# A gated cross-attention block with an fp8 feed-forward on one core: attention stage rebuilt, mean shift added at the output, w_linear's waits moved

## What is computed

```
query  = ctx @ Wq.T + bq                      # ctx: (4, 256, 128)
key    = ctx @ Wk.T + bk
attn   = softmax(query @ key.T)               # (4, 256, 256)
x = x + tanh(g_xattn) * (layernorm(x) @ attn.T)          # x: (4, 256 tokens, 256)
h = layernorm(x)
act = gelu(fp8(h) @ fp8(w_gating[0])) * (fp8(h) @ fp8(w_gating[1]))
x = x + tanh(g_ffn) * (fp8(act) @ fp8(w_linear))         # hidden size 1024
```

## Time and profile before

| what | us |
|---|---|
| median of 3 timed runs (56.16 to 57.09) | 56.71 |
| span of the profiled execution | 54.7 |
| PE busy | 43.6 (80%) |
| DVE busy | 39.6 (72%) |
| POOL busy | 30.7 (56%) |
| ACT busy | 29.6 (54%) |

### The profile page before, as it was taken

One profiled execution on the slowest core, in us unless ns is written; L12 is line 12 of the kernel. 1 busy time (PEld: TensorE's weight loads), 2 busy tenths in 40 slices (PEclk: granted clock), 3 DMA queues, 4 the chain that ended last, 5 costly groups with the idle time before them and its releaser, 6 DMA issues.

```text
span 54.7 us, 874 instructions
## 1 busy us (share of the span) xinstructions
PE 43.6 (80%) x245; PEld 28.7 (53%) x245; DVE 39.6 (72%) x113; ACT 29.6 (54%) x67; POOL 30.7 (56%) x57
## 2 busy tenths in 40 slices
PE   1999999919999401998289999999999999998200
PEld 0338888707888101983234364664564668884000
DVE  1110099999960059998999999949998599889930
ACT  4413636597897930633148966697444693555000
POOL 4109700079992009889898889888884079302200
PEclk9999999999999999999999999999999999999997
DMA  0597999999999700000000000000000003520063
GB/s 0 142 296 175 361 337 263 192 201 204 196 200 279 310 9 0 0 0 0 6 0 0 0 12 0 6 0 0 0 6 0 0 0 113 181 102 0 0 252 131
DMA packets 3461, 5.43 MB, mean 99 GB/s; under 512 B 384, under 2 KB 1792, under 8 KB 3456
## 3 DMA queue, kind: packets, MB, share of 16 engines
q1 hardware_dynamic: 2880, 4.85, 27.0%
q0 software_dynamic: 576, 0.52, 10.3%
HBM read 5.90 MB, written 1.05 MB: 127 GB/s over the span
## 4 chain that ended last, share of the span: by engine, by line
PE 36%; DMA 23%; DVE 13%; SPq 11%; issue 5%; ACT 5%; POOL 1%; DVEq 1%; ACTq 0%
DMA wl<-w_linear 23%; PE bank L686 12%; PE bank L711 11%; PE bank L692 11%; SPq L227 5%; SPq L219 3%; DVE x L483 3%; DVE aq L527 3%; DVE st L488 2%; SPq L217 2%; ACT gl L397 2%; DVE xh L502 2%; PE bank L668 2%; POOL r L274 1%; ACT ys L405 1%
## 5 line engine op out<-in xcount | busy, mean ns | idle before, releaser
L397 ACT ACTIVATE gl<-bank 128x512 bf16<-128x512 f32 (+1 forms) x20 | 10.0, 509 | 6.4 <-PE bank L686 6.4
L518 DVE SCALAR_TENSOR_TENSOR ap<-bank,gl 128x512 f16<-128x512 f32 (+1 forms) x20 | 11.5, 577 | 2.2 <-PE bank L692 1.5
L711 PE MATMUL bank<-wl_q,aq 128*128 128x256 bf16 x64 | 10.1, 273 | 0.8 <-DVE aq L527 0.6
L686 PE MATMUL bank<-xq,wg 128*128 128x512 fp8e4 (+1 forms) x40 | 10.2, 337 | 0.2 <-ACT xq L388 0.2
L692 PE MATMUL bank<-xq,wg 128*128 128x512 fp8e4 (+1 forms) x40 | 10.2, 337 | 0.0
L527 DVE TENSOR_SCALAR aq<-ap 128x512 uint16<-128x512 uint16 (+1 forms) x20 | 8.5, 430 | 0.0
L711 PEld LDWEIGHTS bank<-wl_q,aq 128*128 128x128 f16 x64 | 5.8, 97 | 4.7 <-DVE aq L527 2.3
L646 PE MATMUL bank<-attnT,xT_sb 128*128 128x256 f32 x32 | 8.1, 385 | 0.0
L302 POOL TENSOR_TENSOR wl_sum<-wl_big,wl 128x256 f32<-128x256 f32 x8 | 5.9, 734 | 0.5
L618 PE MATMUL bank<-ident,attn 128*128 128x128 f32 x16 | 2.5, 280 | 4.5 <-POOL attn L283 3.3
L307 POOL TENSOR_TENSOR wl_q<-wl_sum,wl_big 128x256 bf16<-128x256 f32 x8 | 5.8, 728 | 0.5
(11 more groups left out here) (54 smaller groups left out, 69.8 us busy)
## 6 DMA issues: line engine op xcount, KB each, us to landing
x_sb<-x SPq DMA_DIRECT2D x4, 256.0 KB, 5.0
wl<-w_linear SPq DMA_DIRECT2D x2, 512.0 KB, 10.0
xT_sb<-xT SPq DMA_DIRECT2D x4, 256.0 KB, 11.0
out<-yo SPq DMA_DIRECT2D x6, 128.0 KB, 1.9
wg<-w_gating POOLq DMA_DIRECT2D x4, 128.0 KB, 10.1
par<-params_ctxT SPq DMA_DIRECT2D x1, 258.0 KB, 2.7
par<-params_ctxT SPq DMA_DIRECT2D x1, 256.0 KB, 4.5
out<-yo SPq DMA_DIRECT2D x1, 256.0 KB, 2.0
```

Of the source, the lines that this page charges most:

```text
L397: nc.scalar.activation(gl[:, s % 2, toks], gate_b[s % 2][:, toks], ACT.Gelu_apprx_tanh).then_inc(gelu_ready, 1)
L518: nc.vector.scalar_tensor_tensor(ap[:, s % NAP, toks], up_b[s % 2][:, toks], ACT_SCALE, gl[:, s % 2, toks], ALU.mult, ALU.mult).then_inc(p ...
L686: mm = nc.tensor.matmul(gate_b[s % 2][:, toks], wg8[:, c, k, 0, o:o + P], xq[:, g, k, toks], start=(k == 0), stop=(k == KC - 1))
L711: mm = nc.tensor.matmul(halves(y_b[g][i])[:, t], aq[:, s % NAQ, m:m + P], wl_q[:, j], start=(j == 0 and t == 0), stop=(j == HT - 1), skip_ ...
```

## The change

- SyncE loads x and xT of batches 0 and 1, then of 2 and 3, then both halves of w_linear. GpSimd's w_gating loads wait for xT of batch 0.
- The projections of batches 2 and 3 are one product of 512 columns each. k of batches 0 and 1 leaves PSUM on VectorE, one `k_out` of 512 columns and all of q on ScalarE.
- `bn_stats` runs once per batch over the two halves interleaved (512 elements); its even and odd parts are the two tokens' statistics, so no `bn_aggr` follows. The variance is taken from the sum of squares by 1/D.
- `xs` is gone: x2 = s1 * product + x, without the shift. nms1 is added at the output: as the bias of `scale_out`, which now writes each half by itself, and for three halves by `shift_x2` on GpSimd.
- Normalisation of attn: batch 0 on VectorE, 1 to 3 on GpSimd. ve2 and nm2 of batches 2 and 3 are made on GpSimd.
- `wl_constant` runs on ScalarE, for two slices at a time, after the second `xq_out` and among the first gelus. `wl_exponents` stand behind `norm2(1)` and behind step 2 of the feed-forward.
- The orders on all engines are written anew; attend is no longer split around other work.

```diff
-            for b in range(B):
+            for b in (0, 1):
                 sp.dma_start(x_sb[:, b], x[b]).then_inc(s_x[b], 16)
-
-            def load_w_linear(h):
+            for b in (0, 1):
+                sp.dma_start(xT_sb[:, b], xT[b]).then_inc(s_xT[b], 16)
+            for b in (2, 3):
+                sp.dma_start(x_sb[:, b], x[b]).then_inc(s_x[b], 16)
+            for b in (2, 3):
+                sp.dma_start(xT_sb[:, b], xT[b]).then_inc(s_xT[b], 16)
+            for h in range(2):
                 half = slice(h * HT // 2, (h + 1) * HT // 2)
                 sp.dma_start(wl32[:, half], w_linear[:, half]).then_inc(s_wl[h], 16)
-
-            load_w_linear(0)
-            for b in range(B):
-                sp.dma_start(xT_sb[:, b], xT[b]).then_inc(s_xT[b], 16)
-            load_w_linear(1)
...
+            def scales1(h):
+
+                bs = slice(2 * h, 2 * h + 2)
+                pool.wait_ge(st1_ready, 2 * h + 2)
+                nc.gpsimd.tensor_scalar(ve1[:, bs], st1[:, bs, :, 2], 1.0 / D, EPS, ALU.mult,
+                                        ALU.add).then_inc(ve1_ready, 1)
+                pool.wait_ge(ve1_ready, h + 1)
+                nc.gpsimd.tensor_tensor(r1[:, bs], ve1[:, bs], neg_half[:, bs], ALU.pow).then_inc(r1_ready, 1)
+                pool.wait_ge(r1_ready, h + 1)
                 pool.wait_ge(ntg_ready, 1)
-                nc.gpsimd.tensor_scalar(nr1[:, :, :], r1[:, :, :], ntg[:, 0:1], None, ALU.mult).then_inc(nr1_ready, 1)
-                nc.gpsimd.tensor_scalar(s1[:, :, :], r1[:, :, :], tg[:, 0:1], None, ALU.mult).then_inc(s1_ready, 1)
+                nc.gpsimd.tensor_scalar(s1[:, bs], r1[:, bs], tg[:, 0:1], 1.0, ALU.mult,
+                                        ALU.mult).then_inc(s1_ready, 1)
...
+            def shifts1():
+                nc.gpsimd.tensor_scalar(nr1[:, :, :], r1[:, :, :], ntg[:, 0:1], 1.0, ALU.mult,
+                                        ALU.mult).then_inc(nr1_ready, 1)
                 pool.wait_ge(nr1_ready, 1)
-                nc.gpsimd.tensor_tensor(nms1[:, :, :], nr1[:, :, :], mv1[:, :, :, 0], ALU.mult).then_inc(nms1_ready, 1)
+                nc.gpsimd.tensor_tensor(nms1[:, :, :], nr1[:, :, :], st1[:, :, :, 1], ALU.mult).then_inc(nms1_ready, 1)
 
             def rstd2(b):
+                if b >= 2:
+                    pool.wait_ge(st2_ready, b + 1)
+                    nc.gpsimd.tensor_scalar(ve2[:, b], st2[:, b, :, 2], 1.0 / D, EPS, ALU.mult,
+                                            ALU.add).then_inc(ve2_ready, 1)
+                    nc.gpsimd.tensor_scalar(nm2[:, b], st2[:, b, :, 1], -1.0, 1.0, ALU.mult,
+                                            ALU.mult).then_inc(nm2_ready, 1)
                 pool.wait_ge(ve2_ready, b + 1)
...
+            def shift_x2(b, t):
+
+                pool.wait_ge(nms1_ready, 1)
+                pool.wait_ge(x2_ready, LT * b + t + 1)
+                nc.gpsimd.tensor_scalar(x2s[:, b, t], x2[:, b, t], 1.0, nms1[:, b, t:t + 1], ALU.mult,
+                                        ALU.add).then_inc(x2s_ready, 1)
+
...
-            def wl_constant(c):
-                pool.wait_ge(wl_exp_ready, 2 * c * WLC // HT + 1)
-                nc.gpsimd.tensor_scalar(wl_tile(wl_big, c), wl_tile(wl_exp, c), WL_SLOPE, WL_OFFSET, ALU.mult,
-                                        ALU.add).then_inc(wl_big_ready, 1)
-
             def wl_up(c):
-                pool.wait_ge(wl_big_ready, c + 1)
+                pool.wait_ge(wl_big_ready, c // WLB + 1)
...
             def round_wl(c):
-                wl_constant(c)
                 wl_up(c)
                 wl_down(c)
 
-
-            pool.wait_ge(s_ctx[1], 16)
+            nc.gpsimd.memset(wl_offset[:, :], WL_OFFSET).then_inc(offset_ready, 1)
+            pool.wait_ge(s_xT[0], 16)
             for c in range(NWG):
                 load_w_gating(c)
             pool.wait_ge(consts_ready, 1)
-            scales1()
-            shift_x(0)
-            shift_x(1)
-            wl_constant(0)
-            normalise(B - 1)
-            wl_up(0)
+            scales1(0)
+            normalise(1)
+            scales1(1)
+            normalise(2)
+            normalise(3)
             rstd2(0)
-            wl_down(0)
-            wl_constant(1)
             rstd2(1)
-            wl_up(1)
-            wl_down(1)
-            round_wl(2)
+            round_wl(0)
             rstd2(2)
-            round_wl(3)
-            wl_constant(4)
-            wl_up(4)
+            round_wl(1)
             rstd2(3)
-            wl_down(4)
-            for c in range(5, HT // WLC):
+            shifts1()
+            for c in range(2, HT):
                 round_wl(c)
+            for b, t in ((2, 0), (3, 0), (3, 1)):
+                shift_x2(b, t)
             for k in range(LT * GB):
                 add_residual(k)
-
-            pool.wait_ge(scaled_ready, GB + 1)
+            pool.wait_ge(scaled_ready, LT * GB + 1)
             nc.gpsimd.tensor_tensor(yo[:, 2, 1], ys[:, 2, 1], x2[:, 2, 1], ALU.add).then_inc(pool_y_ready, 1)
...
+            def wl_constant(h):
+
+                act.wait_ge(wl_exp_ready, h // 2 + 1)
+                rows = slice(WLB * h, WLB * (h + 1))
+                nc.scalar.activation(wl_big[:, rows].rearrange("p j d -> p (j d)"),
+                                     wl_exp[:, rows].rearrange("p j d -> p (j d)"), ACT.Identity,
+                                     bias=wl_offset[:, 0:1], scale=WL_SLOPE).then_inc(wl_big_ready, 1)
+
+            def scale_out(b, t):
                 g, i = divmod(b, GB)
                 act.wait_ge(ffn2_done, last_step(b) + 1)
-                if b == 0:
+                if b == 0 and t == 0:
                     act.wait_ge(yscale_ready, 1)
-                nc.scalar.activation(ys[:, b].rearrange("p t d -> p (t d)"), y_b[g][i][:, :], ACT.Copy,
+                    act.wait_ge(nms1_ready, 1)
+                nc.scalar.activation(ys[:, b, t], halves(y_b[g][i])[:, t], ACT.Identity, bias=nms1[:, b, t:t + 1],
                                      scale=yscale[:, 0:1]).then_inc(scaled_ready, 1)
...
             q_out(0)
-            k_out(0)
             q_out(1)
-            k_out(1)
+            exps(0)
             q_out(2)
             k_out(2)
-            exps(0)
-            q_out(3)
-            k_out(3)
             exps(1)
             attn_out(0)
             exps(2)
+            attn_out(1)
             exps(3)
-            attn_out(1)
+            nc.scalar.activation(table[:, :], tg[:, 0:1], ACT.Gelu_apprx_tanh)
             attn_out(2)
-
-            nc.scalar.activation(table[:, :], tg[:, 0:1], ACT.Gelu_apprx_tanh)
-            shift_x(2)
+            xq_out(0)
             attn_out(3)
-            shift_x(3)
-            xq_out(0)
             xq_out(1)
+            act.wait_ge(offset_ready, 1)
+            wl_constant(0)
             for s in range(S):
                 gelu(s)
+                if s == 0:
+                    wl_constant(1)
+                if s in (3, 4):
+                    wl_constant(s - 1)
                 if s == X_AFTER[0] - 2:
                     norm2(2)
...
+            def k_out(c):
+                b0, b1 = PROJ[c]
+                dve.wait_ge(k_done, c + 1)
+                nc.vector.tensor_scalar(kT[:, b0 * L:b1 * L], k_b[c][:, 0:(b1 - b0) * L], bk, None,
+                                        ALU.add).then_inc(k01_ready, 1)
...
             def stats1(b):
                 dve.wait_ge(s_x[b], 16)
-                for t in range(LT):
-                    nc.vector.bn_stats(st1[:, b, t], x_sb[:, b, t]).then_inc(st1_ready, 1)
-                for t in range(LT):
-                    dve.wait_ge(st1_ready, LT * b + t + 1)
-                    nc.vector.bn_aggr(mv1[:, b, t], st1[:, b, t]).then_inc(mv1_ready, 1)
+                nc.vector.bn_stats(st1[:, b].rearrange("p t s -> p (t s)"),
+                                   x_sb[:, b].rearrange("p t d -> p d t")).then_inc(st1_ready, 1)
...
+                dve.wait_ge(s1_ready, b // 2 + 1)
                 for t in range(LT):
-                    nc.vector.scalar_tensor_tensor(x2[:, b, t], halves(pv_b[b % 2])[:, t], s1[:, b, t:t + 1], xs[:, b, t],
-                                                   ALU.mult, ALU.add).then_inc(x2_ready, 1)
...
-            def stats2(b, t):
-                dve.wait_ge(x2_ready, LT * b + t + 1)
-                nc.vector.bn_stats(st2[:, b, t], x2[:, b, t]).then_inc(st2_ready, 1)
-
-            def moments2(b):
-                for t in range(LT):
-                    dve.wait_ge(st2_ready, LT * b + t + 1)
-                    nc.vector.bn_aggr(mv2[:, b, t], st2[:, b, t]).then_inc(mv2_ready, 1)
-                dve.wait_ge(mv2_ready, LT * (b + 1))
...
+                    nc.vector.scalar_tensor_tensor(x2[:, b, t], halves(pv_b[b % 2])[:, t], s1[:, b, t:t + 1],
+                                                   x_sb[:, b, t], ALU.mult, ALU.add).then_inc(x2_ready, 1)
+
+            def stats2(b):
```

(98 more changed lines are left out.)

107 lines of the change are left out of this document (45 added, 62 removed).

## The result

| | before | after |
|---|---|---|
| median, us | 56.64 (56.16 to 57.09, 4 runs) | 60.16 (59.52 to 60.38, 4 runs) |
| ratio after / before | 1 | 1.062, 95% interval 1.051 to 1.072 |
| span of the profiled execution | 54.7 | 58.5 |
| energy(0) starts on TensorE | 6.66 | 7.03 |
| first FFN product (T0) | 28.08 | 28.25 |

A forecast was written before the change was run, and what follows sets the result against it. Bound: VectorE's wait for w_linear in attention, then TensorE with GpSimd's rounding just beside it. Span 54.7 + 3.8 for the later eighth slice = 58.5 us, 60.5 with the 2.0 around it; range 57.2 to 62.3.

The forecast's parts named there:

- T0: Start of the first FFN product on TensorE: forecast 27.85 against 28.08, bounds -0.2 and +1.5.
- the five waits: TensorE in attention: 0.9 for each copy of turns 1 and 2, 1.05 norm2(0), 1.4 xq(0)/attnT(3), 0.8 xq(1); 5.0 us.
- B: Rival, not slower: VectorE's 3.83 us wait on w_linear comes off T0 in full, giving 24.25; 56.9 us; chance 0.12.
- C: Rival, faster: B, and GpSimd's rounding without hand-offs, eighth slice ready at 39.9; 54.9 us; chance 0.07.
- The unknown costs: Operations not in the trace: interleaved bn_stats taken as 0.75 us (up to 1.5), wl_constant on ScalarE as 0.60 (to 0.68).
- D: Rival: strided statistics, the interleaved bn_stats, run at half speed; 62.0 us; chance 0.10.
- The rounding: GpSimd's w_linear slices, counted from T0: 17.6 us against 13.6 before; eighth slice ready at 45.5, +3.8 us.
- 16 sums and differences at 0.81 start to start: GpSimd's rounding of eight slices: 0.73 and a hand-off for each operation, 12.96 us in all.
- a sign of error (closer than 1.5): On GpSimd, wl_q pairs closer than 1.5 us would show the forecast wrong; it counted 1.62 a slice.
- E: Rival: GpSimd gives way to VectorE's aq (0.28 undisturbed) in ten steps, +2.8; 63.3 us; chance 0.05.
- E's sign: On GpSimd, a wl_sum over 0.8 us would show E.
- The tail: From the eighth slice to the end: 13.0 us as before; split ys on ScalarE 0 to 0.5, taken as 0.

The follow-up runs named there:

- e7: Changed kernel with only invert_sum(3) moved ahead of add_attention(1) on VectorE: 58.91 us, ratio 1.037.
- e8: Changed kernel with only attnT(3) (attn_out(3)) moved ahead of the first xq on ScalarE: 58.29 us, ratio 1.021.
- e4: Kernel before with one line moved: wl_exponents(1) behind norm2(1) instead of ahead of invert_sum(3) on VectorE: 53.37 us, ratio 0.940.
- e3: Changed kernel without rounding w_linear: GpSimd converts each slice in one operation, right after the first two powers; ratio 0.999.
- e5: Changed kernel with both lines moved, invert_sum(3) ahead of add_attention(1) and attnT(3) ahead of the first xq: 57.41 us, ratio 1.012.
- e10: Kernel before with wl_exponents(1) moved behind moments2(3) at step 2 of the feed-forward: 54.22 us, ratio 0.955.
- e1: Changed kernel with w_linear's rounding moved ahead: early exponents and two constants, four slices before batch 3's small work; ratio 1.003.

## Why the prediction was right

**T0: nearly no change, right.** The forecast laid the stage out from energy(0) at 6.66 and came to 21.19 us from there; 21.22 were measured. The stations between agree too. ScalarE's copy of turn(1), VectorE's reciprocal for batch 3 and ScalarE's copy of turn(3):

```profile
16.70 0.58 ACT L378 COPY attnT<-bank 128x512 f32<-128x512 f32 x1 [1.36 <-PE bank L634]
```

```profile
21.10 0.16 DVE L480 RECIPROCAL rsum<-esum 128x2 f32<-128x2 f32 x1
```

```profile
24.71 0.58 ACT L378 COPY attnT<-bank 128x512 f32<-128x512 f32 x1
```

They end 10.25, 14.23 and 18.26 us behind energy(0); the forecast had 10.19, 14.09 and 18.29. Only the five waits, a figure that its sum does not use, were put too long (5.0 against 4.0). The stage started 0.37 later, so T0 was 28.25, not 27.85. e7 and e8 show that two of the named waits were real ones; the others (copies of turned attn, xq(1)) stand in the timeline above, but no run took them away. Of the rivals with an earlier T0 (B and C), e4 shows that most of B's gain was there to be had, in the old order: its T0 is 18.10 us from energy(0), where B's 24.25 is 17.59. The new order stayed at 21.22, and at 19.38 with both of its places repaired.

**The unknown costs.** An interleaved `bn_stats` takes 0.69 us, so the nearest row, the pair at 0.75, was the right one and D (half speed) fell:

```profile
10.52 0.69 DVE L470 BATCH_NORM_STATS2 st<-x_sb 128x6 f32<-128x512 f32 x1
```

`wl_constant` on ScalarE took 0.71, not 0.60, and lies above the upper end that was given (0.68). It did not delay the first sum against the forecast:

```profile
28.09 0.71 ACT L405 ACTIVATE wl_big<-wl_exp,wl_offset 128x512 f32<-128x512 f32 x1
```

It starts 0.16 ahead of T0, behind the same `xq`, which the forecast had not counted; the two misses cancel, and the first sum followed T0 by 0.63 (forecast 0.65).

**The rounding: the right mechanism, some terms mis-sized.** T0 to the end of the eighth slice was 16.88 us against 17.6:

| term | forecast | measured |
|---|---|---|
| T0 to the first sum | 0.65 | 0.63 |
| slices 0 and 1 | 3.24 | 3.22 |
| rstd2(2) | 1.65 | 1.37 |
| rstd2(3) | 1.65 | 1.93 |
| shifts1 | 0.70 | 0.53 |
| slices 2 to 7 | 9.72 | 9.20 |

The step that was off most is "16 sums and differences at 0.81 start to start". A difference still started 0.80 behind its sum, but the next slice's sum only 0.68 behind the difference (36.73 to 37.41). Slices 2, 3 and 4 thus came 1.48 to 1.49 us apart, which the forecast had called a sign of error (closer than 1.5); that bound was set too tight, on a pattern of before in which another operation always stood between. The forecast's word against rival C, that every pair of neighbours in the trace shows 0.81, was wrong too: before, the difference of slice 0 started 0.70 behind the power ahead of it (22.48).

```profile
23.18 0.73 POOL L307 TENSOR_TENSOR wl_q<-wl_sum,wl_big 128x256 bf16<-128x256 f32 x1
```

What sets the gap is not shown. That a sum does not need the difference ahead of it is not enough: before, a constant did not need it either, and stood 0.81 behind it (38.84 to 39.65).

The two `rstd2` met their 3.3 us together only because one was 0.28 short and the other 0.28 long. The long one is rival E in small: GpSimd gave way to VectorE. The power of batch 3, 0.71 elsewhere, took 1.25 (33.89, above) while VectorE's exponents of the second half ran:

```profile
34.42 0.69 DVE L515 TENSOR_SCALAR wl_exp<-wl 128x1024 int32<-128x1024 int32 x1
```

In e3, which has no such exponents, the same power took 0.71:

```profile
31.91 0.71 POOL L284 TENSOR_TENSOR r<-ve,neg_half 128x2 f32<-128x2 f32 x1
```

The price is 0.54 us, once in the execution. e5, e7 and e8 show it again, with a power of 1.25; each time it ended 0.03 to 0.04 us behind the exponents. E's own place, ten steps of `aq`, showed as sums of 0.84, 0.77 and 0.78 instead of 0.72 in the last three slices, 0.2 us in all against the rival's 2.8. The first of them is over the 0.8 that the forecast had named as E's sign. It started 0.03 us behind an `aq` that kept its 0.28:

```profile
40.40 0.28 DVE L534 TENSOR_SCALAR aq<-ap 128x512 uint16<-128x512 uint16 x1
```

```profile
40.43 0.84 POOL L314 TENSOR_TENSOR wl_sum<-wl_big,wl 128x256 f32<-128x256 f32 x1
```

The Trainium skill, SBUF — State Buffer, Who interferes with whom, says that the engine that comes second blocks fully, whichever it is. The trace agrees in direction for this sum, with GpSimd as second, and for VectorE as second in the earlier trace rows. For the power it does not: by the rows the power started first (33.89) and the exponents second (34.42), and it was the power that grew.

**The tail: mis-sized by 0.3 us.** The forecast gave the split `ys` 0 (bound 0.5), "ScalarE has room". In the chain they stand with most of their time:

```profile
46.84 0.93 ACT ys L415 x2
...
48.00 0.74 ACT ys L415 x2
```

Before, it was one operation of 0.68. The gelu of a half step queues behind each pair. The last slice to the end took 13.37 instead of 13.03. TensorE's first half step and its last instruction, and below them its last instruction before:

```profile
47.02 0.38 PE L705 MATMUL bank<-xq,wg 128*128 128x256 fp8e4 x2
...
54.90 0.39 PE L730 MATMUL bank<-wl_q,aq 128*128 128x256 bf16 x2 [0.73 <-DVE aq L534]
```

```profile
51.12 0.39 PE L711 MATMUL bank<-wl_q,aq 128*128 128x256 bf16 x2 [0.65 <-DVE aq L527]
```

From one to the other it is 7.88 us now and was 7.57 before (from 43.55). All seven kernels with the new output have 7.87 or 7.88, e3 without any rounding too; e4 and e10, with the old one, have 7.56 and 7.57. So the 0.3 us belong to the new output and not to the rounding. That the split `ys` makes them is argued from the chain and not shown: the first `aq` of a half step also took 0.71 in place of 0.41, and no run took the split away.

**The sum.** The eighth slice came 3.46 later (forecast 3.8) and the tail is 0.34 longer (forecast 0), 3.8 us together. That the span met 58.5 to the tenth is luck: T0 0.40 later than forecast (0.37 of it ahead of energy(0), which the change did not make), the rounding 0.72 shorter and the tail 0.34 longer cancel. The 2.0 us around the span were 1.7 to 1.9 in the four executions of the changed kernel (60.29 for 58.5). Of the 3.46, 0.17 come from T0 and 3.29 from the rounding; e1, which starts it early, gave back 2.9 of what lies behind T0.

## What to carry to other kernels

A chain that another engine runs only just ahead of its use must be counted from the moment it may start: tying it to a later event costs it its head start, and that can be more than is won by making its own work shorter. A removed wait is worth its length only if the order behind it has no new hand-offs in it; lay that order out instruction by instruction before crediting the gain. Try the wait alone first: here one moved line made the kernel 6% faster, and the rebuild, in which the same wait is gone, made it 6% slower.
